# Order of the feed-forward steps: z's second half behind its first, two bank pairs in the first group, the normalisation ahead of z low, the feature products one step later

## What is computed

```python
x = L0_attn_x                                   # 4 x 1024 x 512, f32
x = x + _layernorm(_L0_attn_ref(_layernorm(x), Wq, Wk, Wv, Wo))
x = x + _layernorm(_L0_ffn_ref(_layernorm(x), gate_cp, up_cp, down_cp))

def _L0_ffn_ref(hidden_states, gate_cp, up_cp, down_cp):
    gate_w = spline_reconstruct(gate_cp, 2048, 512)
    up_w = spline_reconstruct(up_cp, 2048, 512)
    down_w = spline_reconstruct(down_cp, 512, 2048)
    gate = einsum('bsh,ih->bsi', hidden_states, gate_w)
    up = einsum('bsh,ih->bsi', hidden_states, up_w)
    return einsum('bsi,hi->bsh', silu(gate) * up, down_w)
```

## Time and profile before

| | |
|---|---|
| median of 3 runs | 758.27 us (756.85 to 761.68) |
| the profiled execution | 758.16 us, span 756.4 us |
| TensorE busy | 676.6 us, 89% of the span |
| VectorE busy | 512.7 us, 68% |
| ScalarE busy | 365.5 us, 48% |
| GpSimd busy | 430.7 us, 57% |
| granted TensorE clock | 0.955 |

### The profile page before, as it was taken

The page is one execution under the profiler, slowest core; times in us unless marked ns, Lnnn a source line. Parts: engine busy times, 40 slices in busy tenths (PEclk is TensorE's granted clock), DMA queues, the critical chain, the costliest instruction groups (busy, mean ns, idle before and its releaser), DMA issues. The chain is left out here.

```text
span 756.4 us, 16316 instructions
## 1 busy us (share of the span) xinstructions
PE 676.6 (89%) x5872; PEld 476.1 (63%) x5872; DVE 512.7 (68%) x993; ACT 365.5 (48%) x635; POOL 430.7 (57%) x615
## 2 busy tenths in 40 slices
PE   5996799999999999989947699898989899898996
PEld 3685686878687887867723255565655566564565
DVE  7666773588646973575656668887878878774653
ACT  3532232333232432333335677776777677574641
POOL 5269858547681958910425556564656546554642
PEclk9899899999999999999967899999999999998999
DMA  6814547324561447411786827567394946548123
GB/s 228 309 56 156 182 169 249 119 77 144 190 217 59 159 159 250 138 53 25 209 219 188 186 66 178 131 178 172 123 191 134 206 120 183 123 120 183 63 71 98
DMA packets 65549, 114.98 MB, mean 152 GB/s; under 512 B 12624, under 2 KB 29136, under 8 KB 65488
## 3 DMA queue, kind: packets, MB, share of 16 engines
q1 hardware_dynamic: 65488, 114.16, 52.4%
HBM read 81.76 MB, written 32.37 MB: 151 GB/s over the span
## 5 line engine op out<-in xcount | busy, mean ns | idle before, releaser
L1328 POOL TENSOR_TENSOR act<-inter,act 128x512 f16<-128x512 f32 x128 | 149.6, 1169 | 135.1 <-ACT act L1369 135.0
L1373 ACT ACTIVATE gated<-gbank,c_gate 128x512 f32<-128x512 f32 x128 | 88.0, 687 | 104.0 <-PE gbank L1542 104.0
L1442 DVE SCALAR_TENSOR_TENSOR inter<-ubank,c_up,gated 128x512 f32<-128x512 f32 x128 | 95.6, 747 | 49.8 <-ACT gated L1373 47.8
L1583 PE MATMUL ybank<-down,act 128*128 128x160 f16 x512 | 112.2, 238 | 0.0
L1584 PE MATMUL ybank<-down,act 128*128 128x160 f16 x512 | 111.5, 237 | 0.0
L1585 PE MATMUL ybank<-down,act 128*128 128x160 f16 x512 | 111.4, 236 | 0.0
L1369 ACT CAST act<-inter 128x512 f16<-128x512 f32 x128 | 78.2, 611 | 1.7 <-DVE inter L1442 1.7
L1583 PEld LDWEIGHTS ybank<-down,act 128*128 128x128 f16 x512 | 50.7, 99 | 39.2 <-issue 35.4
L1542 PE MATMUL gbank<-z,s_all 128*32 128x512 f16 x512 | 53.3, 407 | 24.3 <-DMA z<-token_features 15.9
L1542 PE MATMUL ubank<-z,s_all 128*32 128x512 f16 x512 | 52.7, 402 | 8.3 <-DVE inter L1442 7.5
L1584 PEld LDWEIGHTS ybank<-down,act 128*128 128x128 f16 x512 | 51.0, 100 | 3.8
(11 more groups left out here) (195 smaller groups left out, 1943.5 us busy)
## 6 DMA issues: line engine op xcount, KB each, us to landing
x_ln<-x SPq DMA_DIRECT2D x64, 256.0 KB, 3.5
z<-token_features SPq DMA_DIRECT2D x64, 256.0 KB, 5.9
job<-job_in SPq DMA_DIRECT2D x24, 640.0 KB, 4.3
shared<-x SPq DMA_DIRECT2D x32, 256.0 KB, 2.7
x<-shared SPq DMA_DIRECT2D x32, 256.0 KB, 2.0
token_features<-z_hi SPq DMA_DIRECT2D x32, 256.0 KB, 4.2
x_res<-x SPq DMA_DIRECT2D x32, 256.0 KB, 2.7
out<-x_res SPq DMA_DIRECT2D x32, 256.0 KB, 2.1
```

Of the source, the lines that this page charges most:

```text
L1328: pool.tensor_tensor(hidden[par][:, i, TOK:2 * TOK], inter[:, i % INTERS, :], hidden[par][:, i, 0:TOK], ALU.subtract).then_inc(inter_ready, 1)
L1373: act.activation(gated[:, slot % 2, :], gbank[:], ACT.Silu, scale=c_gate[:]).then_inc(silu_done, 1)
L1442: dve.scalar_tensor_tensor(out=inter[:, i % INTERS, :], in0=ubank[:], scalar=c_up[:], in1=gated[:, i % 2, :], op0=ALU.mult, op1=ALU.mult). ...
L1583: pe.matmul(out, hidden[par][:, r, high], box[:, 0], start=False, stop=False)
```

## The change

Four things are moved. `regroup` handles one half at a time: the first in the second quad (spill, then load), the second in the third quad, behind that quad's outputs. In the first group, where ybank is not in use, odd steps put gate and up into its two banks, and a step waits for the bank's use two steps ago; silu then waits on its own for the slot of `gated`. The normalisation of the next tile goes ahead of `z_low` in the fourth step, and the high part of that tile moves from the first step of the next quad to the fourth step, ahead of `z_high`. The feature products move from the end of the third step into the fourth, behind its gate and up.

```diff
+        def pair_of(n):
+
+            return ybank if isinstance(n, int) and n < I and n % 2 else (gbank, ubank)
...
-            def regroup(g, par, loads_before):
-
-
-                for half in range(2):
-                    sp.wait_ge(z_loaded[1 - par][half], loads_before * 64)
-                    feats.spill(sp, half, g, 1 - par)
-                for half in range(2):
-                    ffn_in.load_z(sp, feats, g, par, half)
+            def regroup(g, par, half, loads_before):
+
+
+                sp.wait_ge(z_loaded[1 - par][half], loads_before * 64)
+                feats.spill(sp, half, g, 1 - par)
+                ffn_in.load_z(sp, feats, g, par, half)
...
-                if j == 1 and not (isinstance(g, int) and g == GROUPS - 1):
-                    regroup(g + 1, 1 - par, count)
+                if j in (1, 2) and not (isinstance(g, int) and g == GROUPS - 1):
+                    regroup(g + 1, 1 - par, j - 1, count)
...
             def silu_at(n, slot):
                 act.wait_ge(gate_done, n + 1)
-                act.activation(gated[:, slot % 2, :], gbank[:], ACT.Silu, scale=c_gate[:]).then_inc(silu_done, 1)
+                if isinstance(n, int) and 2 <= n < I:
+                    act.wait_ge(inter_done, n - 1)
+                act.activation(gated[:, slot % 2, :], pair_of(n)[0][:], ACT.Silu, scale=c_gate[:]).then_inc(silu_done, 1)
...
-                    if s == 0 and made:
-                        feats.high(act, g * Q + j + AHEAD)
+                    if s == 3 and begun:
+                        feats.high(act, g * Q + j + AHEAD + 1)
                     if s == 3 and made:
                         feats.z_high(act, g * Q + j + AHEAD, (j + 2) % Q, g + 1, z_banks, par if j < 2 else 1 - par)
...
+                    if s == 3 and begun:
+                        feats.norm(dve, m + 1, (j + 1 + AHEAD) % RING)
                     if s == 3 and made:
                         feats.z_low(dve, m, (j + 2) % Q, z_banks, par if j < 2 else 1 - par)
-                    if s == 3 and begun:
-                        feats.norm(dve, m + 1, (j + 1 + AHEAD) % RING)
...
+                first = isinstance(n, int) and n < I
+                gate, up = pair_of(n)
+                for w, bank, free, done in ((GATE, gate, silu_done, gate_done), (UP, up, inter_done, up_done)):
+                    if not first:
                         pe.wait_ge(free, n)
+                    elif n >= 2:
+                        pe.wait_ge(free, n - 1)
...
+                    if s == 3 and made:
+                        feats.products(pe, m, z_banks)
                     if i == 0 and not first:
                         moment_pair(g - 1, I // 2 - 1, 1 - par)
...
-                    if s == 2 and made:
-                        feats.products(pe, m, z_banks)
```

More of the change, by code:

```diff
@@ L1422, in _ @@
             high(0, 0, 0, 0)
+            feats.high(act, Q + 2)
             feats.z_high(act, Q + 1, 1, 1, z_banks)
@@ L1441, in product @@
                     dve.wait_ge(inter_ready, n - INTERS + 1)
-                dve.scalar_tensor_tensor(out=inter[:, i % INTERS, :], in0=ubank[:], scalar=c_up[:],
+                dve.scalar_tensor_tensor(out=inter[:, i % INTERS, :], in0=pair_of(n)[1][:], scalar=c_up[:],
                                          in1=gated[:, i % 2, :], op0=ALU.mult, op1=ALU.mult).then_inc(inter_done, 1)
@@ L1512, in _ @@
             feats.stats(dve, Q + 2, 2, 2)
+            feats.norm(dve, Q + 2, 2)
             feats.z_low(dve, Q + 1, 1, z_banks)
-            feats.norm(dve, Q + 2, 2)
             schedule(dve, quad)
@@ L1536, in gate_up @@
                 side, c = i // HALF, i % HALF
-                for w, bank, free, done in ((GATE, gbank, silu_done, gate_done), (UP, ubank, inter_done, up_done)):
-                    if not (isinstance(n, int) and n == 0):
+                first = isinstance(n, int) and n < I
+                gate, up = pair_of(n)
+                for w, bank, free, done in ((GATE, gate, silu_done, gate_done), (UP, up, inter_done, up_done)):
+                    if not first:
                         pe.wait_ge(free, n)
+                    elif n >= 2:
+                        pe.wait_ge(free, n - 1)
                     for u in range(4):
```

## The result

The changed kernel takes 771.59 us (median of 4 runs, 769.67 to 773.53), the kernel before, in runs beside it, 759.97 (756.85 to 762.63). The ratio is 1.0166, with an interval of 1.0121 to 1.0210: slower by 1.7%. The forecast of 764 was 7.6 us too low; the time lies in the range of 747 to 776, and the change was slower by more than 1%, which had 0.35 against 0.43 for no change. The profiled execution took 773.53 us with a span of 771.7, against 758.16 and 756.4.

What follows compares the result with a forecast made beforehand. TensorE bounds the four full groups; after the change a ring through VectorE and ScalarE would. First group 0, next stretch +2.7, four groups +7.1, last stretch -4.2: +5.6 on 758.16 gives 764 us, range 747 to 776.

Steps and rivals of the forecast that it cites:

- The ring: Feed-forward quads: VectorE and ScalarE wait on each other through normalisation, h_hi, z_hi, z_lo and h_lo; 10.9 us a quad, was 9.86.
- the row of x_res: Profile row for VectorE's output step: x_res ends 0.54 us after GpSimd's subtraction; the same was taken for a blocked h_lo.
- Between the groups: Quad between two groups: the moments' two low parts, 0.60 us each, come on top, making 12.1 us.
- rival (c): Feed-forward quads: TensorE idles more and its clock falls; 11 falls at 1.2 us on top of the forecast, 777 us; chance 0.14.
- The last stretch: Stretch from 641.88 us: waits and clock falls go, longer quads and moments come; 56.43 to 52.2 us, so -4.2.
- the first half's way: From first spill of z to TensorE having it: 14.74 us shrinks to 10.3 to 12.7, ending six of seven waits.
- The longer quads: In the last stretch, two quads lengthened by the change were to add 2.1 us.
- The ring through ubank: Feed-forward quads: the fourth step's up matmuls wait for VectorE's third product to free ubank; 10.27 us a quad against 9.86.
- Bank pairs and the first group: First group: most of nine ubank waits, 7.5 us, end, but one chain limits it; change 0, bounds -4 and +3.
- (a): VectorE in each quad: h_lo slips in ahead of the subtraction; quad 10.3 to 10.55 us, total 753 us; chance 0.27.
- (b): Feed-forward half: TensorE stays the bound and the z waits vanish; quad 9.6 us, total 732 us; chance 0.08.
- Rival (d): Group ends: the first half of z comes no earlier; 5 waits stay at 1.5 us, total 771 us; chance 0.08.

## Why the prediction was right, and where its sizes were off

**The ring is right, to 0.1 us.** From the product of the second step to the end of z_hi the prediction had 8.02 + 0.1; the quad shown has 565.60 - 557.50 = 8.10. From there to the next such product it had 2.84; measured 568.39 - 565.60 = 2.79. The twelve ordinary quads of the four groups take 10.98 us in the mean against 10.9, which is 0.9 us in all. h_lo ends 0.55 us after the subtraction (568.47 and 567.92), as the row of x_res had it. The Trainium skill (SBUF — State Buffer, section Who interferes with whom) says that the one that comes second fully blocks; read strictly, h_lo would have taken its full 0.69 us after that and ended 0.14 later, and the measurement decides for the row. Swapping h_hi and z_hi takes the ring away and 25.7 us with it, and undoing the whole step takes 30. Cutting the one subtraction gives 5: the port is a smaller part, the queue of ScalarE the larger.

**Between the groups: mis-sized, and the largest error.** The step put two moments at 0.60 on top, 12.1 us. Measured are 12.79, 13.30, 12.79 and 13.40: 52.3 against 48.4, +3.9 us. First, and in all four, h_lo is pushed back by moment and eviction of y until the subtraction of the next product lies over it; at a full clock the quad is then 12.79, 0.7 more than the sum had (VectorE, GpSimd and TensorE in one such quad):

```profile
532.20 0.69 DVE L1453 SCALAR_TENSOR_TENSOR mom_lo<-mbank,mom_hi 128x512 f16<-128x512 f32 x1 [0.15 <-ACT mom_hi L1383]
532.80 0.74 DVE L1461 TENSOR_SCALAR y<-ybank,c_out 128x512 f32<-128x512 f32 x1
533.46 1.56 DVE L1051 SCALAR_TENSOR_TENSOR h_lo<-xn,h_hi 128x512 f16<-128x512 f32 x1
```
```profile
533.33 1.15 POOL L1330 TENSOR_TENSOR act<-inter,act 128x512 f16<-128x512 f32 x1 [0.43 <-ACT act L1371]
```
```profile
535.08 0.61 PE L1073 MATMUL turned<-ident,h_hi 128*128 128x128 f16 x4 [1.65 <-DVE h_lo L1051]
```

Then TensorE's clock falls in every second of these quads. Why not in the others stays open: the two with a fall wait 1.65 us for h_lo, the others 1.64 and 1.61. The kernel with one subtraction cut waits 1.62 to 1.65 in these quads without any fall, so the length of this wait does not settle it. Two of them, the same work at 0.87 and at 1.00:

```profile
531.21:544.51 13.30, 11.16 (x126) 6.65 (x126) 11.11 (x19) 7.35 (x14) 6.21 (x9) 0.87 0.59 139
577.52:590.31 12.79, 9.97 (x126) 6.26 (x126) 10.82 (x19) 7.58 (x14) 6.61 (x9) 1.00 0.54 142
```

It costs 0.5 to 0.6 us a time, since the ring leaves TensorE idle time that hides the rest. That is as much of rival (c) as came: two falls in the four groups, where it was to decide from eight falls.

**The last stretch: mis-sized.** It was to fall by 4.2 us, to 52.2, and fell by 1.3, to 55.1. The step that failed is the first half's way at 10.3 to 12.7 us. SP and TensorE:

```profile
691.46 0.45 SPq L998 DMA_DIRECT2D token_features<-z_hi  x1
...
697.52 1.80 SPq L1146 DMA_DIRECT2D z<-token_features  x4
```
```profile
705.55 0.62 PE L1551 MATMUL gbank<-z,s_all 128*32 128x512 f16 x4 [2.92 <-DMA z<-token_features]
```

The way is 14.09 us here. Four loads are issued in 1.80 us as foreseen, but they start only 6.06 us after the first spill and have landed 8.03 us after that; the time does not go with the bytes ahead. So 2.92 us are waited for instead of 1.5, and the clock falls after it (0.86 from 701.08 to 713.68, 12.60 x 0.14 / 0.5 = 3.5 us at the lower level, at most 1.8 lost). The longer quads were too low as well: the one with the second moment took 12.75 us, and the lighter one behind it 10.10 instead of 9.43, for which the sum had nothing. One slip goes the other way: by its own 0.91 this stretch had 56.43 x 0.09 / 0.5 = 10.2 us at the lower level, which costs up to 5.1, and the prediction took off only two falls at 1.7. In the other six places the wait did vanish, because the quads are longer; with the quads of before it shrinks to between 0 and 1.25 us there.

**Products behind gate and up: right.** The ring through ubank was worked out at 10.27 us, and is 10.20 to 10.24 wherever nothing longer covers it. It was right, too, that this is slower than 9.86 inside a group. What I did not see is that the move is a help to the early normalisation: 20.5 us with h_hi ahead (792.1 to 771.6), 19.2 with h_hi behind (765.1 to 745.9), and 2.5 without (744.0 to 741.5, not to be told from nothing). It brings the fourth step's gate forward by 1.4 us and so the normalisation mostly out from under the subtraction (0.72 us instead of 1.32).

**Bank pairs and the first group: nothing, as a sum of two that cancel.** The forecast of 0 stands at +1.2. Split, pairs and moved products bring the first group from 42.8 to 40.9, 39.6 and 37.1 us in turn, and the early normalisation takes it to 44.0; the bounds of -4 and +3 held neither part alone, so that the sum came near 0 is luck. Not all nine waits for ubank stood in this group, as the prediction has it: the ninth, of 0.39 us, comes at 437.75, in the next stretch. I take the 1.1 us ahead of the first gate as scatter: over the twelve kernels this gate starts between 388.6 and 391.8, in no order with their edits.

The sum of the errors: 4.8 in the four groups, 2.9 in the last stretch, 1.2 in the first group, 1.1 ahead of it, -0.2 in the second stretch and -0.1 behind: 9.7 us against the profiled execution, 7.6 against the median. That is more than the 5.6 us of change that was forecast: the direction was right because the ring was, not because the sum was close. One mechanism fell, the way of z that goes with the bytes ahead of it. Rivals (a) and (b) fell, as h_lo came behind the subtraction, by 0.14 us in the quad shown, and TensorE did wait for ubank. Rival (d) fell in the four groups.

Of the edits, the split of z is what is worth having, 16.5 us alone. The early normalisation, with its high part ahead of z_hi, costs 30 and hides that gain.

## What to carry to other kernels

Before an instruction is moved up a queue that runs in order, ask what independent work is queued behind it and what it waits for: h_hi filled no gap, it handed VectorE's lateness to z_hi, and swapping the two neighbours was worth 3%. When edits come in a bundle, cost each alone and time each alone; a gain of 2% lay under a loss of 4%. An idle gap in front of an instruction can be what keeps another engine's work out of its neighbour's way, so look at what runs beside the gap before filling it.

## What was not expected of the hardware

The normalisation reads one tensor of SBUF where h_lo and x_res read two, and is held by GpSimd's subtraction too: 1.32 us instead of 0.54 when it starts 0.12 us behind it. It ends 0.28 us after the subtraction (564.74 and 564.46), and as much after the pair of subtractions in the changed kernel (563.97 and 563.68); h_lo and x_res end 0.54 to 0.55 after.

The split of z shortened the way of the first half by only 0.8 to 1.6 of 14.7 us where it is waited for, although three of ten transfers no longer stood ahead of it.
